# A mixture-of-experts kernel: the second slice's row scatter on GpSimd in six short bursts, each behind one result of the first slice

## What is computed

```python
h = _layernorm(x) * (1 + ca) + sa
x = x + ga * attn(h)            # scan over 256 time steps, 16 heads
h = _layernorm(x) * (1 + cb) + sb
logits = h @ router_w + router_b
route = softmax(logits); max_prob = max(route); max_ind = argmax(route)
for e in range(8):
    a, g = split(h @ w1[e], 2)              # 128 -> 2 * 512
    y = silu(a) * g @ w2[e]                 # 512 -> 128
    out = where(max_ind == e, y, out)
x = x + gb * out * max_prob
```

## Time and profile before

| | us |
|---|---|
| timed executions, median of 3 | 491.53 |
| span of the profiled execution, first to last instruction | 487.9 |
| PE busy | 377.1 (77%) |
| DVE busy | 383.3 (79%) |
| ACT busy | 277.9 (57%) |
| POOL busy | 263.1 (54%) |

### The profile page before, as it was taken

How to read it: one execution, slowest core, us unless ns; L and a number is a source line. 1 busy time by engine, 2 the same in 40 slices (tenths; PEclk the granted TensorE clock), 3 DMA queues, 4 the chain that set the end, 5 groups by cost and what they waited for, 6 DMA issues and landing times.

```text
span 487.9 us, 8633 instructions
## 1 busy us (share of the span) xinstructions
PE 377.1 (77%) x2505; PEld 325.1 (67%) x2505; DVE 383.3 (79%) x1166; ACT 277.9 (57%) x624; POOL 263.1 (54%) x325
## 2 busy tenths in 40 slices
PE   2967763956799978948779588699997779999970
PEld 1322312754678568938669578598997678999960
DVE  5778999999999999999979997749664224468624
ACT  3697967756474666766466353548454354555520
POOL 1127238999999678576772884022216663333340
PEclk9978995978889997987976869989999977999995
DMA  8177799990000019431000011341131122414006
GB/s 227 41 101 125 109 118 151 103 69 1 1 0 1 2 18 388 114 57 31 0 2 0 13 39 51 75 88 35 39 114 38 50 78 56 130 42 130 29 27 177
DMA packets 49309, 35.00 MB, mean 72 GB/s; under 512 B 10992, under 2 KB 45584, under 8 KB 49136
## 3 DMA queue, kind: packets, MB, share of 16 engines
q1 hardware_dynamic: 45424, 28.28, 30.7%
q0 software_dynamic: 3264, 5.92, 4.0%
q10 hardware_dynamic: 576, 0.26, 0.2%
HBM read 15.26 MB, written 10.27 MB: 52 GB/s over the span
## 4 chain that ended last, share of the span: by engine, by line
DVE 33%; PE 31%; POOL 13%; issue 11%; ACT 5%; DMA 2%; another core or an unknown queue 2%; ACTq 1%; SPq 0%; POOLq 0%; DVEq 0%
PE bank L839 12%; PE bank L854 5%; DVE U L1682 5%; DVE S L1695 5%; DVE p L1676 4%; DVE p L1689 4%; PE bank L650 4%; POOL big L950 2%; DVE big L1612 2%; PE bank L738 2%; DVE X L1614 2%; PE bank L593 1%; PE bank L654 1%; POOL X L918 1%
## 5 line engine op out<-in xcount | busy, mean ns | idle before, releaser
L1052 POOL DMA_INDIRECT placed_y<-Q,place x46 | 44.1, 958 | 101.9 <-DVE place L1888 38.1
L839 PE MATMUL bank<-Q,p 128*128 128x128 f32 x736 | 97.2, 281 | 2.2 <-ACT p L1399 2.2
L650 PE MATMUL bank<-prod_o,ID 128*128 128x128 f32 x512 | 75.4, 308 | 29.0 <-POOL prod_o L294 17.1
L839 PEld LDWEIGHTS bank<-Q,p 128*128 128x128 f32 x736 | 92.1, 197 | 2.6 <-ACT p L1399 2.4
L650 PEld LDWEIGHTS bank<-prod_o,ID 128*128 128x128 f32 x512 | 70.4, 219 | 31.8 <-POOL prod_o L294 20.3
L1210 ACT ACTIVATE p<-S,GAM 128x64 f32<-128x64 f32 x126 | 48.3, 410 | 65.4 <-DVE S L1695 64.6
L287 POOL TENSOR_TENSOR prod_o<-Q,ST 128x1024 f32<-128x1024 f32 x28 | 60.0, 2141 | 29.6 <-PE bank L654 17.1
L1399 ACT ACTIVATE p<-big 128x1024 f32 x46 | 48.5, 1057 | 44.4 <-PE bank L839 30.7
L1695 DVE TENSOR_REDUCE S<-p 128x64 f32<-128x320 f32 x126 | 56.6, 488 | 0.0
L1682 DVE TENSOR_REDUCE U<-p 128x32 f32<-128x288 f32 x128 | 53.0, 454 | 0.0
L1676 DVE TENSOR_TENSOR p<-S,bank 128x256 f32<-128x256 f32 x128 | 49.7, 423 | 0.7 <-ACT bank L1205 0.7
(11 more groups left out here) (253 smaller groups left out, 740.4 us busy)
## 6 DMA issues: line engine op xcount, KB each, us to landing
big<-in_L_ffn_w_dram SPq DMA_DIRECT2D x1, 4096.0 KB, 14.1
big<-big SPq DMA_DIRECT2D x16, 192.0 KB, 5.0
Q<-sorted_h SPq DMA_DIRECT2D x46, 64.5 KB
sorted_h<-ZERO SPq DMA_DIRECT2D x2, 1472.0 KB, 19.4
X<-in_L_attn_x_dram SPq DMA_DIRECT2D x8, 256.0 KB, 4.4
big<-big SPq DMA_DIRECT2D x16, 128.0 KB, 5.2
K<-placed_y SPq DMA_DIRECT2D x8, 256.0 KB
out_dram<-X SPq DMA_DIRECT2D x8, 256.0 KB, 2.3
```

Of the source, the lines that this page charges most:

```text
L650: pe.matmul(ps, ID[:, :], prod_o[:, k % 2, i, :], start=(i == 0), stop=False, skip_group_check=True)
L839: m = pe.matmul(bank[(1, 6)[g % 2] + k][:, c * P:(c + 1) * P], W1E[g % 2][:, f:f + P], XST[:, g % 3, :], start=True, stop=True)
L1052: pool.indirect_dma_start(placed_y[g // NF], bass.IndirectOffsetOnAxis(ap=place[:, g:g + 1], axis=0), YS[:, g % YR, :], None).then_inc(sem ...
```

## The change

The table `BURSTS` gets a row for each slice. The first slice keeps its three bursts. The second slice's 16 tiles go in bursts of 3, 3, 3, 3, 2 and 2. The bursts are no longer sent in one go at g = 10: burst k is sent after result 10 + k, so results 11 to 15 stand between the bursts where they stood behind them. The wait for all 16 landings moves behind result 16, and the wait for result 15's own landing is gone.

```diff
-    BURSTS = (0, 6, 11, NT)
+    BURSTS = ((0, 6, 11, NT), (0, 3, 6, 9, 12, 14, NT))
@@ def sort_rows(s, burst)
-                first, end = BURSTS[burst:burst + 2]
+                first, end = BURSTS[s][burst:burst + 2]
@@ for g in range(NTIME * NF), on POOL
-                if g == SCAT:
-                    for burst in range(len(BURSTS) - 1):
-                        sort_rows(1, burst)
+                if SCAT <= g < SCAT + len(BURSTS[1]) - 1:
+                    sort_rows(1, g - SCAT)
+                if g == SCAT + len(BURSTS[1]) - 1:
                     pool.wait_ge(sem("scattered", 1), 16 * NT)
-                if g in (SCAT + 5, SCAT + 10):
+                if g == SCAT + 10:
                     pool.wait_ge(sem(f"ys_out{g % YR}"), 16 * (g // YR + 1))
```

## The result

The changed kernel takes 494.28 us (median of 12 runs, 492.84 to 496.44); the kernel before, run beside it, 491.35 us. The ratio is 1.0087 with an interval of 1.0061 to 1.0113: slower by 0.9%, about 3 us. The profiled execution's span is 493.6 us. The runs of the changed kernel list time and span together (495.35 and 493.6, 493.76 and 492.0), so 1.75 us lie around a span, not 3.6; the profiled execution of the kernel before took about 489.7 us. One execution against one, the difference is 5.7 us, of which the medians show half.

What follows compares the result with a forecast made beforehand. PE was taken to set the pace, losing 9.4 us to late results over tiles 16 to 22. 487.9 + 0 + 0 + 0, with 3.6 around the span, gave 491.5, stated as 491.9; range 487.4 to 496.6.

Steps and rivals of the forecast that it cites:

- unchanged pace: Main case: tiles 16 to 22 keep their present 28.9 us; chance 0.35, range of its own 490.6 to 492.8.
- unbroken row: Rival: filling the holes between POOL's bursts, which let PE's results through, loses 4.4 us, giving 495.9; chance 0.28.
- Slower: Outcome class: the changed kernel measures slower than the kernel before; chance 0.39, against same 0.32 and faster 0.29.
- the turn of tile 23: Sign: PE's turn of tile 23 stays at 404.7; the prediction is wrong if it moves by more than 1 us.
- the late results of PE: Term for tiles 16 to 22, where PE's results reach other engines 3 to 5 us late: taken as unchanged, 0.
- Bursts and handovers: Step on POOL's row bursts: second burst near 372.0, last row tile issued at 393.2 in place of 388.56, 4.6 us later.
- Results 11 to 15 go earlier: Term on POOL: these results issue at about 370.5 to 390.4, none makes POOL wait; worth nothing.
- Rows covered: Term: rows landing later lie beside PE's work, tile 23 in SBUF at 398.9, needed at 404.73; cost 0, cover 5.9 us.
- The backlog: Term on POOL's results behind the rows: seven in place of 12 to catch up, until about 404; worth nothing by itself.
- The rule of the Trainium skill: Cited rule: DMA never contends with a compute engine; PE's late results would have nothing to do with POOL's row.
- What lies around the span: Term for the time between profiled span and measured median: 3.6 us, added to 487.9 to give 491.5.

Runs made afterwards that it cites:

- e11: Changed kernel with two tiny waited-for writes on POOL behind every second-slice row DMA and behind results 11 to 26, nothing reordered: 492.91 us, ratio 1.0006 to the kernel before.
- e1: Changed kernel, but each burst after the first also waits for the landing of the result sent just ahead of it: 489.55 us, ratio 0.9938 to the kernel before.
- e2: Kernel before with the second slice's rows in the six short bursts, one after the other, no result between them: 488.43 us, ratio 0.9892.
- e5: Kernel before with two tiny waited-for writes on POOL behind every row DMA of the second slice, bursts 6, 5, 5 kept: 488.47 us, ratio 0.9946.
- e7: Kernel before with rows in six short bursts and the twelve results behind them in pairs, each pair waiting for its landing: 488.02 us, ratio 0.9957.
- e8: Kernel before with rows in four bursts of four and the results behind them in pairs, each pair waiting for its landing: 486.47 us, ratio 0.9924.
- e10: Kernel before with rows in two bursts of eight, two waited-for writes behind each row DMA and behind results 11 to 26: 488.10 us, ratio 0.9892.
- e12: Changed kernel with one tiny waited-for write on POOL behind every second-slice row DMA and behind results 11 to 26: 494.51 us, ratio 1.0049 to the kernel before.
- e9: Kernel before with one waited-for write behind each row DMA, bursts 6, 5, 5, and two behind results 11 to 26: 487.18 us, ratio 0.9886.
- e6: Kernel before, but POOL sends the second slice's 16 row tiles as plain DMAs of the same size, unsorted: 483.76 us, ratio 0.9845.
- e3: Kernel before, but SP stores the second slice's 16 row tiles as plain DMAs of the same size, unsorted; POOL issues no rows there: 476.63 us, ratio 0.9659.

## Why the prediction was right or wrong, point by point

- The range, 487.4 to 496.6, held 494.28, because it had been drawn wide enough for the rivals. The forecast itself, 491.9 by unchanged pace, did not come true: the *unbroken row* rival with its 495.9 is what happened. Slower had the largest of the three chances, 0.39, but the text put its likeliest single case elsewhere. By its own sign, the turn of tile 23 at 404.7 to within 1 us, the prediction is wrong: the turn came at 411.41.
- The step that failed is *the late results of PE*, taken at 0. Tile 22 moved from 398.63 to 406.34, 7.7 us, of which 1.0 was there before the change had begun (`pos` at 367.3 for 366.3): a term of 6.7 us in the profiled execution. I had chosen 0 because the load looked nearly equal, with a mean spacing of 1.54 us that was to become 1.32 (that is 17% more DMAs per time, not 14). The mean is too coarse a measure: the experiments show that the pause from one indirect DMA to the next counts, and whether there are long ones among them. The holes, which the rival named, were worth more than its upper bound of 4.4 us: a tile could take 11.4 us, not 5.8. Some 1.1 us of it are the slower clock behind PE's long hole, for which the prediction had no term.
- 2.0 us of it came back. From tile 22's silu to tile 23's it is 9.2 us before and 7.2 after. PE's clock was granted at 0.65 in that stretch before and at 1.00 after, and the products show it: from the last group of L854 to tile 23's turn it is 1.87 us before (402.86 to 404.73) and 0.99 after (410.42 to 411.41). The sum, 6.7 + 1.0 - 2.0 = 5.7 us, is the difference of the spans.
- *Bursts and handovers*: with `pos` 1.04 us later, the second burst was due at 373.0 and came at 372.84; right. The last row tile was due at 394.2 and came at 395.99, SP's load was due at 396.8 and came at 398.39. The 1.7 us come from POOL's wait for DVE at result 14, 2.94 us. *Results 11 to 15 go earlier* said that none would make POOL wait; that was read off the old pace of DVE, which the change slowed.
- *Rows covered*: right here, since PE came to the turn at 411.4. The experiments show what a later landing costs without cover: 13.6 us of waiting in e11, where the pauses put it off further, and 5.7 us in e1.
- *The backlog*, worth nothing: wrong as a principle. Its own density makes PE's results late (e2, e5, e7, e8, e10). In the changed kernel it goes out 2.2 to 2.7 us apart from 398.8 to 411.2, and the tiles beside it come in steps of 2.8 us or less.
- *The rule of the Trainium skill* (SBUF — State Buffer, on contention), that DMA never contends with a compute engine and PE waits for nobody's port, doesn't cover this: with only POOL's pause changed, tile 22 moves by 18 us (e11 against the changed kernel). The measurement decides that PE's results are late beside POOL's row; whether a port has a part in it no run here shows.
- *What lies around the span* was taken as 3.6 us and is 1.75, so the sum against the profiled execution's own time was 1.8 us too high.

## What to carry to other kernels

When one engine's results reach all others late by microseconds and no wait in the program explains it, look at what another engine does densely at that time, and test it with the cheapest pause. Holes that a wait leaves in a DMA queue can be what keeps the rest running: filling one with useful issues need not be free, and the mean rate alone doesn't show it. Price a reordering of POOL's indirect DMAs by the shortest and longest pauses between them, in the backlog behind them too, and against the landing that somebody waits for.

## What the runs showed of the hardware that was not expected

- Indirect DMAs issued from POOL with 0.30 us between them (1.26 us from start to start), beside a PE at full demand, go with PE's results reaching the other engines late: by 2 us some 2 us into the row and by 4.7 us a tile later in the kernel before, by up to 13 us in the unbroken row of the changed one. With 0.65 us between them (1.61) the delay is gone (e5, e10, e11). With 0.44 us (1.41) it is nearly whole in the unbroken order (e12) and half gone where two holes are left (e9). Long pauses let the results through.
- Plain DMAs of the same size from POOL, 0.53 us apart, show nothing of it (e6), nor do such plain DMAs issued from SP (e3).
- While PE stood idle for 9.55 us its granted clock was down to 0.50, and the group of eight products behind the hole took 2.07 us in place of 1.06 to 1.15.
- Why PE's results are late stays open, and so does whether the product itself or only word of it is late, since the ends of PE's products are modelled in a trace. The pause was varied, not the path: whether it is the reading of row numbers, the many single rows per DMA or something else in the indirect form wasn't tried. It also stays open how much of PE's own load it needs: the earlier trace rows show none of it beside the first slice's rows, and PE's load wasn't varied.
